# The projection of queries moved from a block of its own into the engine programs of cross attention

## The reference

```python
q = (layernorm(x) @ Wq.T + bq)            # scaled by sqrt(16) = 4
k = ctx @ Wk.T + bk                       # ctx: 32 batches, 1601 keys, 256
v = ctx @ Wv.T + bv
attn = softmax(q k^T * scale) per head    # 16 heads of 16
x = x + (attn @ v) @ Wp.T + bp
x = x + circuit_ffn(layernorm(x))
x = x + experts(x)                        # 1 shared expert, 7 routed, top 2
```

## Time and profile before

| | us |
|---|---|
| median of 3 runs (2079.83 to 2082.58) | 2079.84 |
| the profiled execution | 2082.68 |
| its span, from first to last instruction | 2080.9 |
| projection of queries, to its last store issue | about 51 |
| head of attention, to the first score matmul | 54.6 to 98.2 |
| main loop of attention | 98.2 to about 1490 |

### The profile page before, as it was taken

The page is one execution under the profiler, slowest core; times in us unless marked ns, Lnnn a source line. Parts: engine busy times, 40 slices in busy tenths (PEclk is TensorE's granted clock), DMA queues, the critical chain, the costliest instruction groups (busy, mean ns, idle before and its releaser), DMA issues. The chain is left out here.

```text
span 2080.9 us, 46743 instructions
## 1 busy us (share of the span) xinstructions
PE 1930.5 (93%) x18894; PEld 1806.9 (87%) x18894; DVE 1477.0 (71%) x2802; ACT 1147.2 (55%) x1931; POOL 614.1 (30%) x616
## 2 busy tenths in 40 slices
PE   4599999999999999999999999999559699999998
PEld 2499999999999999999999999999447589999998
DVE  3477777777777777777777777777486556666656
ACT  3165656565665656656566665565474335555552
POOL 0223222232322323222232223320111125677750
PEclk9699999999999999999999999999869799999999
DMA  3666666666666666666666665665201525666533
GB/s 116 174 171 161 170 155 154 160 164 162 158 159 152 175 161 159 156 155 172 162 158 156 158 165 147 176 156 125 75 19 61 172 107 187 210 212 210 198 109 122
DMA packets 152775, 318.33 MB, mean 153 GB/s; under 512 B 58048, under 2 KB 83648, under 8 KB 149104
## 3 DMA queue, kind: packets, MB, share of 16 engines
q1 hardware_dynamic: 148336, 303.80, 53.9%
q0 software_dynamic: 4224, 11.54, 1.8%
HBM read 136.56 MB, written 20.58 MB: 76 GB/s over the span
## 5 line engine op out<-in xcount | busy, mean ns | idle before, releaser
L381 ACT COPY a_pT<-a_pst 128x512 f32<-128x512 f32 x768 | 421.6, 583 | 434.9 <-PE a_pst L599 434.9
L387 ACT ACTIVATE a_probs<-a_probs,a_nmax 128x1601 f32<-128x1601 f32 x256 | 418.8, 1636 | 147.7 <-DVE a_probs L425 147.7
L599 PE MATMUL a_pst<-a_id,a_probs 128*128 128x128 f32 (+1 forms) x3328 | 452.4, 274 | 29.0 <-ACT a_pT L381 26.4
L425 DVE TENSOR_SCALAR_CACHE_REDUCE a_probs<-a_pss 128x1608 f32<-128x1608 f32 x256 | 467.3, 1825 | 14.3 <-PE a_pss L588 12.1
L599 PEld LDWEIGHTS a_pst<-a_id,a_probs 128*128 128x128 f32 (+1 forms) x3328 | 381.9, 141 | 72.3 <-ACT a_probs L387 36.6
L349 POOL TENSOR_TENSOR a_tick<-a_tick 128x1 f32<-128x1 f32 x62 | 12.0, 193 | 978.5 <-DMA a_raw<-in_ctxT 963.1
L443 DVE TENSOR_SCALAR a_khi<-a_psk,a_bk 128x402 fp32r<-128x402 f32 x250 | 158.6, 634 | 143.2 <-PE a_psk L553 138.4
L354 POOL TENSOR_TENSOR a_clo<-a_raw,a_chi 128x402 fp32r<-128x402 f32 x240 | 246.3, 1059 | 4.8
L588 PE MATMUL a_pss<-a_kst,a_bd 96*128 96x402 f32 x1024 | 240.4, 357 | 6.8 <-DVE a_klo L445 6.8
L551 PE MATMUL a_pso<-a_whi,a_chi 128*128 128x256 f32 x806 | 241.0, 299 | 0.0
L553 PE MATMUL a_pso<-a_whi,a_clo 128*128 128x256 f32 x806 | 226.9, 281 | 0.0
(11 more groups left out here) (229 smaller groups left out, 3556.8 us busy)
## 6 DMA issues: line engine op xcount, KB each, us to landing
a_kst<-a_khi SPq DMA_DIRECT2D x1024, 100.5 KB, 2.5
a_kst<-a_klo SPq DMA_DIRECT2D x512, 100.5 KB, 2.6
a_raw<-in_ctxT SPq DMA_DIRECT2D x60, 804.0 KB, 5.5
e_gur<-in_wgu SPq DMA_DIRECT2D x24, 1408.0 KB
e_dr<-in_wd SPq DMA_DIRECT2D x24, 768.0 KB
a_bd<-q_scr SPq DMA_DIRECT2D x192, 32.0 KB, 2.0
e_big<-ys_scr SPq DMA_DIRECT2D x8, 512.0 KB, 7.5
a_pT<-in_ctxT SPq DMA_DIRECT2D x2, 1608.0 KB, 8.1
```

The lines of the kernel that those rows point to most:

```text
L381: nc.scalar.copy(pT[:, p % HALF, 4 * i:4 * i + 4, :], ps_t[:, i % 2, :].rearrange("p (t q) -> p t q", q=P)).then_inc(t_copied_act, 1)
L387: nc.scalar.activation(pr, pr, ACT.Exp, bias=nmax[:, b, p:p + 1], scale=-1.0, accum_out=esum[:, b, p:p + 1]).then_inc(probs_ready, 1)
L425: nc.vector.tensor_scalar(probs[:, p % 2, :].rearrange("p (b k) -> p b k", b=QK), ps_s[:, :, 0:KQ], -1.0, None, ALU.mult, ALU.min, accum_o ...
L599: mm = nc.tensor.transpose(ps_t[0:r, i % 2, (t % 4) * P:(t % 4 + 1) * P], probs[:, p % 2, t * P:t * P + r], id_sb[:])
```

## The change

`project_queries` is gone as a block. Its statements stand at the head of the five engine programs of `cross_attention`, with no meeting of the engines between projection and attention.

- Buffers: `wq_sb` lies in `raw`; `x_sb`, `xT` and the query parts (two slots in place of four groups) lie where `k_st` will be; `qT` lies in slot 1 of `v_sb`. The turned rows go through `ps_t`, `ps_o` and `ps_k`, the product through `ps_s`.
- SP: the loads of x are three (4, 4 and 8 tiles). Wk, Wv and context 0 are issued ahead of the last one. One constant less is loaded (the identity is shared). The stores of group 0 come before the load of context 1, those of group 1 before the fill of the queries of batch 0, and the first stacking of keys waits until all stores have landed.
- ACT: the high part of the weights is made between the turned rows of groups 0 and 1, that of context 0 after the products of groups 1 and 2, one half each.
- DVE: the low part of the weights stands after the normalisation of group 1, that of context 0 after `lower(1)` and `lower(2)`, ahead of the normalisation of group 3 and of `lower(3)`.
- POOL: the zeroing of `bd` stands ahead of the four powers.
- PE: steps 1 to 4 of batch 0 wait until the bank they write has been read by ACT.
- The semaphore on which the last stage waits for its stores is allocated outside.

```diff
-    project_queries(nc, ins["x"], ins["wq"], ins["bq"], ins["ident"], q_scr)
...
+        wq_sb = raw[:, 0:NC * D].rearrange("p (k d) -> p k d", k=NC)
...
+        with ExitStack() as early:
+            sbe = lambda n, s, d=F32: early.enter_context(nc.sbuf_tensor(n, s, d))
+            x_sb, xT = sbe("q_x", [P, NT, D]), sbe("q_xT", [P, NC, TOK])
+            q_hi, q_lo = sbe("q_hi", [P, 2, NC, 512], F32R), sbe("q_lo", [P, 2, NC, 512], F32R)
...
+        qT = v_sb[:, 1].rearrange("p t d -> p (t d)")[:, 0:4 * 512].rearrange("p (i t) -> p i t", i=4)
...
+        row_bank = lambda i: (ps_t[:, 0, :], ps_t[:, 1, :], ps_o[:], ps_k[:])[i % 4]
...
+            def store_queries(g):
+
+                sp.wait_ge(q_split, NC * (g + 1))
+                for i, part in enumerate((q_hi, q_lo)):
+                    sp.dma_start(q_scr[i].rearrange("(m p) t -> p m t", p=P)[:, :, tokens(g)], part[:, g % 2].bitcast(F32)).then_inc(stored[min(g, 2)], 16)
+
+            load_x(0, slice(0, GT))
+            for dst, src in ((id_sb[:], ident), (wq_sb, wq), (bq_sb[:], bq)):
+                sp.dma_start(dst, src).then_inc(wq_loaded, 16)
+            load_x(1, slice(GT, 2 * GT))
             sp.dma_start(w_raw[:, 0], wk).then_inc(w_loaded, 16)
             sp.dma_start(w_raw[:, 1], wv).then_inc(w_loaded, 16)
             sp.dma_start(first_ctx[:, 0], ctxT[0]).then_inc(first_loaded, 16)
-            for dst, src in ((bk_sb[:], bk), (bv_sb[:], bv), (wp_sb[:], wp), (bp_sb[:], rows[:, 0]), (id_sb[:], ident)):
+            load_x(2, slice(2 * GT, NT))
+            for dst, src in ((bk_sb[:], bk), (bv_sb[:], bv), (wp_sb[:], wp), (bp_sb[:], rows[:, 0])):
                 sp.dma_start(dst, src).then_inc(const_loaded, 16)
-            sp.wait_ge(bd_zeroed, 1)
-            fill_queries(0, 0)
-
+            store_queries(0)
             sp.wait_ge(first_loaded, 16)
             sp.dma_start(first_ctx[:, 1], ctxT[1]).then_inc(first_loaded, 16)
+            store_queries(1)
+            sp.wait_ge(bd_zeroed, 2)
+            sp.wait_ge(stored[0], 32)
+            fill_queries(0, 0)
+            store_queries(2)
+            store_queries(3)
+
+            sp.wait_ge(stored[1], 32)
+            sp.wait_ge(stored[2], 32 * 2)
             for m, z in ((0, 0), (0, 1), (1, 0)):
                 stack_keys(0, m, z)
...
+            act.wait_ge(bias_ready, 1)
+            copy_rows(0)
+            for g in range(NG):
+                if g == 0:
+                    act.wait_ge(w_loaded, 32)
+                    nc.scalar.copy(w_hi[:], w_raw).then_inc(w_hi_done, 1)
+                if g < NG - 1:
+                    copy_rows(g + 1)
+                for m in range(NC):
...
+                    nc.scalar.activation(qT[:, i % 4, :], ps_s[:, i % 4, :], ACT.Identity, bias=bq_scaled[:, m:m + 1], scale=SCALE).then_inc(q_biased, 1)
+                    act.wait_ge(q_biased, i + 1)
+                    if g > 1 and m == 0:
+
+                        act.wait_ge(stored[g - 2], 32)
+                    nc.scalar.copy(q_hi[:, g % 2, m, :], qT[:, i % 4, :]).then_inc(q_hi_done, 1)
+                if 0 < g <= NC:
+                    act.wait_ge(first_loaded, 16)
+                    nc.scalar.copy(c_hi[:, 0, g - 1, :], first_ctx[:, 0, g - 1, :]).then_inc(ctx0_hi_done, 1)
...
+            for g in range(NG):
+                if g < NG - 1:
+                    sums(g + 1)
+                normalise_rows(g)
+                if g == 1:
+                    dve.wait_ge(w_hi_done, 1)
+                    nc.vector.tensor_tensor(w_lo[:], w_raw, w_hi[:].bitcast(F32), ALU.subtract).then_inc(w_split, 1)
+                if g > 0:
+                    lower(g - 1)
+                if g > 1:
+                    k = g - 2
+                    dve.wait_ge(ctx0_hi_done, k + 1)
+                    nc.vector.tensor_tensor(c_lo[:, 0, k, :], first_ctx[:, 0, k, :], c_hi[:, 0, k, :].bitcast(F32), ALU.subtract).then_inc(ctx0_split, 1)
+            lower(NG - 1)
             dve.wait_ge(const_loaded, 16 * CONSTS)
...
             for s in range(STEPS):
+                if 1 <= s <= QK:
+
+                    pe.wait_ge(q_biased, NC * NG - QK + s)
                 if s > QK:
                     pe.wait_ge(kv_copied, s - QK)
                 step(0, 0, s, first_banks[s % (QK + 1)])
```

More of the change, by code:

```diff
@@ L68, in rows_keys @@
     return P if t < KT - 1 else KTL
[L71 to L215, removed]
@@ L218, in cross_attention @@
-def cross_attention(nc, ctxT, x, q_scr, wk, bk, wv, bv, wp, rows, ident, x1_scr, x1_mv):
+def cross_attention(nc, ctxT, x, q_scr, wq, bq, wk, bk, wv, bv, wp, rows, ident, x1_scr, x1_mv):
     with ExitStack() as ctx:
@@ L247, in cross_attention @@
         ps_s, ps_t, ps_o, ps_k = ps("a_pss", [P, QK, 512]), ps("a_pst", [P, 2, 512]), ps("a_pso", [P, 512]), ps("a_psk", [P, 512])
+        x_all_loaded = [sem(f"q_xl{g}") for g in range(3)]
+        stored = [sem(f"q_stored{g}") for g in range(3)]
+        wq_loaded, bias_ready = sem("q_w_loaded"), sem("q_br")
+        stat_done, aggr_done, var_done, pow_done, norm_done = (
+            sem("q_stat"), sem("q_aggr"), sem("q_var"), sem("q_pow"), sem("q_norm"))
+        q_rows_filled, q_rows_copied, q_filled, q_biased, q_hi_done, q_split = (
+            sem("q_tf"), sem("q_tc"), sem("q_qf"), sem("q_qb"), sem("q_qh"), sem("q_qs"))
         w_loaded, w_hi_done, ctx0_hi_done, ctx0_split = sem("a_wl"), sem("a_wh"), sem("a_c0"), sem("a_c0s")
@@ L388, in exponentials, with copy_rows @@
                                      accum_out=esum[:, b, p:p + 1]).then_inc(probs_ready, 1)
-            act.wait_ge(w_loaded, 32)
-            nc.scalar.copy(w_hi[:], w_raw).then_inc(w_hi_done, 1)
-            act.wait_ge(first_loaded, 16)
-            for k in range(NC):
-                nc.scalar.copy(c_hi[:, 0, k, :], first_ctx[:, 0, k, :]).then_inc(ctx0_hi_done, 1)
+            def copy_rows(g):
+                for k in range(NC):
+                    i = NC * g + k
+                    act.wait_ge(q_rows_filled, i + 1)
+                    nc.scalar.copy(xT[:, k, tokens(g)], row_bank(i)).then_inc(q_rows_copied, 1)
+            act.wait_ge(bias_ready, 1)
[7 more added lines that the diff above has]
+                for m in range(NC):
+                    i = NC * g + m
+                    act.wait_ge(q_filled, i + 1)
+                    if i >= 4:
+                        act.wait_ge(q_split, i - 3)
+                    nc.scalar.activation(qT[:, i % 4, :], ps_s[:, i % 4, :], ACT.Identity, bias=bq_scaled[:, m:m + 1], scale=SCALE).then_inc(q_biased, 1)
[6 more added lines that the diff above has]
+                    nc.scalar.copy(c_hi[:, 0, g - 1, :], first_ctx[:, 0, g - 1, :]).then_inc(ctx0_hi_done, 1)
             def body(it, first):
@@ L492, in residual, with sums, normalise_rows, lower @@
                 nc.vector.bn_aggr(out=x1_mv[:, t, :], in_=x_stats[:]).then_inc(x1_summed, 1)
+            def sums(g):
+                dve.wait_ge(x_all_loaded[min(g, 2)], 16)
+                for t in range(GT * g, GT * (g + 1)):
+                    nc.vector.bn_stats(out=stats[:, t, :], in_=x_sb[:, t, :]).then_inc(stat_done, 1)
+                for t in range(GT * g, GT * (g + 1)):
+                    dve.wait_ge(stat_done, t + 1)
+                    nc.vector.bn_aggr(out=mv[:, t, :], in_=stats[:, t, :]).then_inc(aggr_done, 1)
+                dve.wait_ge(aggr_done, GT * (g + 1))
+                tiles = slice(GT * g, GT * (g + 1))
+                nc.vector.tensor_scalar(vare[:, tiles], mv[:, tiles, 1], EPS, None, ALU.add).then_inc(var_done, 1)
+            def normalise_rows(g):
+                dve.wait_ge(pow_done, g + 1)
+                for t in range(GT * g, GT * (g + 1)):
+                    nc.vector.tensor_scalar(x_sb[:, t, :], x_sb[:, t, :], mv[:, t, 0:1], rstd[:, t:t + 1],
+                                            ALU.subtract, ALU.mult).then_inc(norm_done, 1)
+            def lower(g):
+                for m in range(NC):
+                    i = NC * g + m
+                    dve.wait_ge(q_hi_done, i + 1)
+                    nc.vector.tensor_tensor(q_lo[:, g % 2, m, :], qT[:, i % 4, :], q_hi[:, g % 2, m, :].bitcast(F32), ALU.subtract).then_inc(q_split, 1)
+            sums(0)
+            dve.wait_ge(wq_loaded, 48)
+            nc.vector.tensor_scalar(bq_scaled[:], bq_sb[:], SCALE, None, ALU.mult).then_inc(bias_ready, 1)
             nc.vector.memset(own[:], 0.0).then_inc(own_set, 1)
@@ L627, in project_out, with turn_rows @@
                 mm.then_inc(y_filled, 1)
+            def turn_rows(g):
+                pe.wait_ge(norm_done, GT * (g + 1))
+                for k in range(NC):
+                    i = g * NC + k
+                    if i >= 4:
+                        pe.wait_ge(q_rows_copied, i - 3)
+                    for j in range(GT):
+                        mm = nc.tensor.transpose(row_bank(i)[:, j * P:(j + 1) * P], x_sb[:, GT * g + j, k * P:(k + 1) * P], id_sb[:])
+                    mm.then_inc(q_rows_filled, 1)
```

(18 more changed lines are left out.)

25 lines of the change are left out of this document (16 added, 9 removed).

## The result

The changed kernel takes 2070.48 us (median of 5 runs, 2068.74 to 2070.72) against 2079.84 for the kernel before on the same chip: a ratio of 0.9955, 95% interval 0.9942 to 0.9967. Ten more runs of it, beside fifteen of the kernel before (median 2079.24), gave a median of 2072.16 and a ratio of 0.9969 (0.9956 to 0.9982). Over all fifteen runs its median is 2070.5, over all twenty of the kernel before 2079.5. So it is faster by 0.3 to 0.45%: 9.4 us in the first group of runs, 7.1 in the second, 9.0 over both, where 15.7 were forecast. The time forecast was 2064.1, the range 2059.5 to 2069.5, and the result lies just above it.

What follows compares the result with a forecast made beforehand. PE bounds the main loop, and its idle hole ahead of step 0 (70.44 us) delays the start; first stacking at 62.6 instead of 78.35 gives 2079.84 - 15.7 = 2064.1 us, range 2059.5 to 2069.5.

Steps and rivals of the forecast that it cites:

- What bounds the kernel: PE fills the main loop, so only its start can move; PE's idle hole until step 0 at 70.44 is the target.
- the stretch of 19.9 us: From first stacking (78.35) to first score matmul (98.24), no projection work takes part; carried over unchanged.
- Part 1: Loads of x: the last lands at 18.1, behind weights and context 0, moving turn(1) and product(0) by +5.4 us.
- Part 2: Projection: product to end of lower takes 6.55 us, not 7.7, so lower(0) ends at 29.7, +4.2.
- Part 3: Context 0's low half on DVE delays normalise(3) by +7.5 instead of +4.2; step 0 starts at 56.7.
- The lock: DVE operations with two SBUF inputs wait for POOL's split of context 1: 0.5 us, bounds none to 1.1.
- rival 2: POOL also holds DVE through normalise(3): +4.2 us, 2068.3, up to 2070 with half clock; chance 0.15.
- Part 4: SP's first stacking waits for group 3's stores, 4.3 us after lower(3) ends at 58.3: 62.6.
- The sum against the median: Stacking at 62.6 in place of 78.35 takes 15.7 us off the median 2079.84, giving 2064.1.
- Rival 1: Projection keeps its pace, with x not held back and room on DVE: 24 us gained, 2055.8; chance 0.04.
- Rival 3: Loads share the engines, so x's second load lands with the last: 3 us more, 2067.1; chance 0.09.
- Rivals 4 and 5: Loop: POOL's splits hold DVE's L469, 2118 us, chance 0.03; or the loop swallows the shift, no change, chance 0.02.

Runs made afterwards that it cites:

- e3: Changed kernel with the last load of x issued ahead of the weights and context 0: 2065.04 us, ratio 0.9937.
- e6: Changed kernel with x first, POOL's split late, low halves behind normalise(3), and odd groups' query parts in the probabilities' buffer: 2056.60 us, ratio 0.9891.
- e4: Changed kernel with the low halves of context 0 placed behind normalise(3) and behind lower(2): 2066.33 us, ratio 0.9943.
- e8: The kernel before, profiled once more without any edit: one run, 2078.05 us.
- e5: Changed kernel with x's last load first, POOL's split of context 1 late, and low halves of context 0 behind normalise(3): 2057.59 us, ratio 0.9900.
- e2: Changed kernel with POOL splitting context 1 only after the last low part of the queries: 2067.06 us, ratio 0.9948.
- e10: Changed kernel with each half of context 1's low part in twelve POOL instructions of 134 columns, not four of 402: one run, 2069.01 us.

## Why the prediction was right or wrong

**What bounds the kernel: right.** The hole ahead of step 0, the stretch of 19.9 us carried over, and the loop that passes on the shift all hold.

**Part 1, the loads: right.** In the six traces with the changed order of loads the second load landed at 7.7 to 10.25 and the last at 15.9 to 18.25; 9.64 and 18.1 were assumed. The distance between the two scatters by only 0.2 us, from 8.0 to 8.2, beside the 8.3 worked out from the pace of the slow engine (9.64 and 8.3 make 17.9 and not the 18.1 taken). So the last load does wait behind the 2.1 MB, e3 takes this delay out, and what scatters is when the second load lands.

**Part 2, the rate of a product: right in kind, taken from its better side.** I took 4.44 us. product(0) took 5.54 in the first trace of the changed kernel, 4.51 in the second, and then product(1) 5.57. In nine of the ten traces of the changed kernel and its edits one of the two took 5.2 us or more, 4.90 being the longer one in e6: some 1.1 us is nearly always paid.

**Part 3, the low half ahead of normalise(3): right,** by e4's 2.45 us and by step 0 following ACT and DVE as worked out.

**The lock: this is the step that failed.** I saw it in the earlier trace rows and priced it at 0.5 us, for operations with two tensor inputs, and put normalise, with one tensor input, into rival 2 at a chance of 0.15 and a price of 4.2. It happened in both traces of the changed kernel: 4.85 for 1.38, +3.5 us, plus 0.8 on the low half in the first (0.1 in the second). The rows of before could have told more. There is no case of an SBUF-to-SBUF `TENSOR_SCALAR` beside a busy POOL among my rows, but the trace of before has one: a `TENSOR_SCALAR` of 16 columns, with a constant as its scalar, that lasts 3.95 us (3.70 in e8) and ends 0.5 us behind a POOL memset.

```profile
1500.57 3.51 POOL L817 MEMSET f_hd<- 128x4096 f32 x1
1500.66 3.95 DVE L859 TENSOR_SCALAR f_scl<-f_rs 128x16 f32<-128x16 f32 x1 [2.64 <-POOL f_rs L816]
```

No run varied this pair, but with it normalise belonged into the sum. The Trainium skill, GPSIMD Engine Reference, Key points, names two SBUF inputs and 2-port modes as the cases of contention. Normalise has one tensor input, and alone it shows no sign of a faster mode (0.41 us, as long as the statistics of the same 256 columns). Whether it counts as one of the page's cases the runs can't show; it was held all the same, and the measurement decides.

**Part 4, the last store: its term was 0.8 us too small.** SP went on 5.2 us after the last low part in the first trace, 5.1 in the second, 4.3 assumed: +0.8. e3 shows the same 5.2 with a store issue of 0.47 us, so it isn't the issue of 1.81. Why it is slower than before stays open.

**The sum against the median: a second, quieter error.** I took the shift from one profiled execution and put it on the median. That execution ran more of its K steps at half clock than e8, which begins stacking 1.9 us earlier. A chain that was long by chance in the trace is a gain by chance in the sum. Against the forecast of 62.6, stacking began 3.4 us late in the first trace of the changed kernel. Its terms, as the trace gives them, are 3.5 for normalise, 0.3 for the low half beyond the 0.5 of the sum, 1.1 for the clock in product(0) and 0.9 for the store, less 2.2 for x, which landed early: 3.6. In the second trace it was 5.6 late: 3.5 for normalise, 1.1 for the clock in product(1), 1.2 for that in product(2) and product(3) and 0.8 for the store, less 0.4 for the low half and 0.1 for x: 6.1. Normalise is the largest term both times. From e8's 76.48 the stacking is then 10.5 and 8.3 us earlier, and the times say 9.4 and 7.1.

**The rivals.** Rival 2 is what happened: normalise was held, by 3.5 us where 4.2 were priced. Its 2068.3 is 2 us short of the result; the "up to 2070" given for it with half clock was the nearest number. Rival 1 describes what e5 and e6 reach once its two obstacles are gone (2057.6 and 2056.6 against 2055.8). Rival 3 fell by e3. Rivals 4 and 5 fell: the loop's batches are unchanged. The range ended at 2069.5, just short of that 2070: it held the lock and the clock as nearly alternatives, and normalise's hold came together with the half clock in a product and the longer store.

## What to carry to other kernels

Work that fills the gaps of a serial chain has to stand behind the chain's next link on its engine and not ahead of it, and a load that the chain waits for has to be issued ahead of all that the chain doesn't: here one moved load and two moved groups of statements were worth 11 to 14 us, more than the 7 to 9 that the removed barrier had brought without them. Before work is put on GpSimd beside VectorE, look at each VectorE instruction it will lie beside, and if it is on the chain, move GpSimd's work or cut it small (e2 and e10). And check a profiled execution against the spread of the times before its chain is subtracted from their median.

## What the runs showed of the hardware that I had not expected

A DVE `TENSOR_SCALAR` with one tensor in SBUF and its two scalars from SBUF waits for POOL's running instruction: 0.41 us alone, 1.12 beside pieces of 402 columns, up to 3.73 beside one of 1608, 0.55 beside 134. Beside the long one (3.57 us) it lasted from 47.35 to 51.08 and ended 0.14 us behind it. `TENSOR_SCALAR` with its tensor in PSUM and its scalar in SBUF kept its 0.64 us beside the same split (e2). POOL waits in turn: four pieces that take 4.1 us alone took 6.0.

One execution of the changed kernel lost 3.3 us in the first batch of its loop against another: a wait of PE of 1.9 us, and half clock right behind it. Ten runs of that kernel scatter by 7 us; this batch and the head (2.2 us) make up most of the difference between the two that have a trace.
